# Who issues the regrouping transfers of a self-attention batch: three of six query transfers and two of twelve key transfers go to GpSimd

## The reference

```python
x = x + attn(layernorm(x)); x = x + xattn(layernorm(x), ctx); x = x + ffn(layernorm(x))

def attn(x):                       # 16 heads of 8 channels
    q, k, v = (split_heads(x @ W + b) for W, b in ((Wq, bq), (Wk, bk), (Wv, bv)))
    scores = einsum('bhqd,bhkd->bhqk', q, k) / sqrt(8)
    scores = where(mask, scores, -inf)          # blocks of 64 tokens, and 8 global tokens
    return einsum('bhqk,bhkd->bhqd', softmax(scores), v) @ Wo + bo
```

## Time and profile before

| | |
|---|---|
| median of 3 runs | 567.36 us (565.86 to 570.26) |
| profiled execution | 572.98 us, of which 571.1 us is the span |
| PE / PEld busy | 85% / 64% |
| DVE busy | 71% |
| ACT busy | 52% |
| POOL busy | 51% |
| DMA engines' share in the self attention | 0.38 to 0.61, batch by batch |

### The profile page before, as it was taken

How to read it: one execution, slowest core, us unless ns; L and a number is a source line. 1 busy time by engine, 2 the same in 40 slices (tenths; PEclk the granted TensorE clock), 3 DMA queues, 4 the chain that set the end, 5 groups by cost and what they waited for, 6 DMA issues and landing times. The chain is left out here.

```text
span 571.1 us, 16500 instructions
## 1 busy us (share of the span) xinstructions
PE 487.5 (85%) x5675; PEld 363.8 (64%) x5675; DVE 408.1 (71%) x1245; ACT 297.4 (52%) x757; POOL 288.6 (51%) x540
## 2 busy tenths in 40 slices
PE   1978989899989899878989999999867999999810
PEld 1756666667666666546767777677644888888610
DVE  7567989999888888867987898788472343433337
ACT  2573665555656665425664666465424534444237
POOL 5543434433333343101276788777772477777720
PEclk9997999999999999979997999899988999999985
DMA  6626343545655656216232333322125443343159
GB/s 192 111 53 136 62 63 62 110 107 108 109 108 101 112 103 137 64 47 139 65 80 71 98 85 99 89 73 81 33 67 144 114 113 111 110 115 94 53 173 291
DMA packets 96002, 58.30 MB, mean 102 GB/s; under 512 B 24560, under 2 KB 92224, under 8 KB 95920
## 3 DMA queue, kind: packets, MB, share of 16 engines
q1 hardware_dynamic: 74448, 40.00, 30.3%
q10 hardware_dynamic: 16896, 7.34, 6.5%
q0 software_dynamic: 4576, 9.91, 5.2%
HBM read 20.83 MB, written 17.50 MB: 67 GB/s over the span
## 5 line engine op out<-in xcount | busy, mean ns | idle before, releaser
L507 POOL TENSOR_SCALAR veps<-mv 128x2 f32<-128x2 f32 x48 | 10.8, 225 | 159.3 <-issue 101.4
L1278 ACT ACTIVATE probs<-ps 128x512 f32<-128x512 f32 x128 | 73.2, 602 | 12.1 <-PE ps L1658 10.0
L602 POOL DMA_INDIRECT expert_in<-xn,sloti x64 | 65.6, 1025 | 17.9 <-issue 17.9
L1133 DVE TENSOR_TENSOR eh<-ps,sg 128x256 f32<-128x256 f32 x40 | 17.0, 425 | 59.1 <-ACT sg L1482 58.1
L761 DVE TENSOR_REDUCE nmax<-ps 128x8 f32<-128x512 f32 x64 | 42.5, 686 | 18.9 <-PE ps L1593 18.8
L655 POOL DMA_INDIRECT expert_out<-ey,xt x40 | 38.3, 958 | 27.6 <-DVE ey L1140 17.1
L761 DVE TENSOR_REDUCE mparts<-ps 128x8 bf16<-128x512 f32 x64 | 43.3, 685 | 6.3 <-PE ps L1648 5.9
L1593 PE MATMUL ps<-kbd,qs 96*64 96x128 bf16 x512 | 38.1, 293 | 4.5 <-DMA qs<-part 2.5
L2005 PE MATMUL ps<-wgu,turned 128*128 x160 | 41.2, 380 | 0.0
L1476 ACT COPY turned<-ps 128x512 f32<-128x512 f32 (+1 forms) x43 | 23.8, 554 | 27.7 <-PE ps L1998 23.2
L509 POOL TENSOR_TENSOR rstd<-veps,minus_half 128x2 f32<-128x2 f32 x48 | 35.6, 742 | 4.0
(11 more groups left out here) (247 smaller groups left out, 1387.4 us busy)
## 6 DMA issues: line engine op xcount, KB each, us to landing
kbd<-part SPq DMA_DIRECT2D x192, 32.0 KB
qs<-part ACTq DMA_DIRECT2D x93, 64.0 KB
xt<-expert_in SPq DMA_DIRECT2D x64, 72.0 KB
qs<-part SPq DMA_DIRECT2D x51, 64.0 KB
ck_scr<-wgu SPq DMA_DIRECT2D x6, 512.0 KB
ckbd<-ck_scr SPq DMA_DIRECT2D x16, 192.0 KB
kbd<-part SPq DMA_DIRECT2D x48, 64.0 KB
wgu<-in_L_ffn_gate_up_w SPq DMA_DIRECT2D x4, 512.0 KB, 3.9
```

Source lines behind the costliest of these rows:

```text
L602: pool.indirect_dma_start(xs, bass.IndirectOffsetOnAxis(sloti[b % 3][:, n:n + 1], 0), xn3[b % 3][:, n // TOPK, n % TOPK, :], None).then_in ...
L1278: a_.activation(probs[:, 2 * i:2 * i + 2, :], P2[i % 2][:, :].rearrange("p (j q) -> p j q", j=2), ACT.Exp, scale=SCALE).then_inc(s("probs" ...
```

## The change

From batch 2 on, GpSimd issues five of the 18 transfers: the two query transfers of the second part, the two key transfers of the third part, and the query transfer of the third part, in this order. They add to a semaphore of their own, `lent`. ScalarE keeps the three query transfers of the first part, SP ten key transfers. Whoever waited for `got` now waits for `got` (13 transfers a batch) and `lent` (5). Batches 0 and 1 go as before.

```diff
-        GOT = {True: 16 * 3 * NP, False: 16 * NP}
+        GOT = 16 * NP
+        FIRST_LENT, LENT = 2, 5
+        def self_got(n):
+            return 16 * (3 * NP * n - LENT * max(n - FIRST_LENT, 0))
+        def self_lent(n):
+            return 16 * LENT * max(n - FIRST_LENT, 0)
...
-                        if K_PART[i] == k:
+                        if K_PART[i] == k and (b < FIRST_LENT or k < 2):
                             for a in range(2):
                                 sp.dma_start(kbd[p][16 * i + 8 * a:16 * i + 8 * a + 8, :, a, :, :].rearrange("r j k n -> r j (k n)"),
...
-                wait_apart(sp, (s_("got"), GOT[True] * b + GOT[True]))
+                wait_apart(sp, (s_("got"), self_got(b + 1)), (s_("lent"), self_lent(b + 1)))
...
+            def later_parts_regrouped(b, p):
+                at_least(pool, s_("pair"), 4 * (b - 1))
+                for k in (1, 2):
+                    pool.wait_ge(s_("part"), 3 * b + k + 1)
+                    for i in range(NP):
+                        if Q_PART[i] == k:
+                            pool.dma_start(qs[p][16 * i:16 * i + 16, :, :], part[:, k, 0:S]).then_inc(s_("lent"), 16)
+                        if K_PART[i] == k == 2:
+                            for a in range(2):
+                                pool.dma_start(kbd[p][16 * i + 8 * a:16 * i + 8 * a + 8, :, a, :, :].rearrange("r j k n -> r j (k n)"),
+                                               part[64 * a:64 * a + 64, k, S:2 * S]).then_inc(s_("lent"), 16)
...
             def self_body(b, p):
                 if has(b + 1):
                     self_global_heads(b + 1, 1 - p)
+                    if b + 1 >= FIRST_LENT:
+                        later_parts_regrouped(b + 1, 1 - p)
...
-                at_least(act, s_("got"), GOT[True] * b)
+                at_least(act, s_("got"), self_got(b))
+                at_least(act, s_("lent"), self_lent(b))
                 a_.copy(part[:, 0, :], qk[p][:, :]).then_inc(s_("part"), 1)
...
-                if b != 1:
+                if b == 0:
                     queries_regrouped(b, p, 1)
...
                     self_second_part(b + 1, 1 - p)
-                    if b > 0:
-                        queries_regrouped(b + 1, 1 - p, 2)
...
-                    pe.wait_ge(s_("got"), GOT[True] * b + GOT[True])
+                    pe.wait_ge(s_("got"), self_got(b + 1))
+                    at_least(pe, s_("lent"), self_lent(b + 1))
```

More of the change, by code:

```diff
@@ L432, in regroup_cross @@
                              ck_scr[:, :, :, 2 * M * b:2 * M * (b + 1)].rearrange("i r j n -> (i r) j n")).then_inc(w_("ck_put"), 16)
-                sp.wait_ge(c_("got"), GOT[False] * (b + 1))
+                sp.wait_ge(c_("got"), GOT * (b + 1))
             sp.wait_ge(w_("laid_out"), 2)
@@ L1290, in cross_first_part @@
                 if b == 0:
-                    act.wait_ge(s_("got"), GOT[True] * B)
-                at_least(act, c_("got"), GOT[False] * (b - 1))
+                    act.wait_ge(s_("got"), self_got(B))
+                    act.wait_ge(s_("lent"), self_lent(B))
+                at_least(act, c_("got"), GOT * (b - 1))
                 at_least(act, c_("part"), 3 * b)
@@ L1639, in cross_scores @@
                     pe.wait_ge(w_("ck_put"), 16 * (NP + b + 1))
-                    pe.wait_ge(c_("got"), GOT[False] * (b + 1))
+                    pe.wait_ge(c_("got"), GOT * (b + 1))
                     if b == 0:
```

## The result

The changed kernel takes 572.71 us (median of six runs, 571.63 to 579.89), the kernel before 566.84 (six runs, 565.86 to 570.26): 1.0102 times as long, 95% interval 1.0056 to 1.0149. It is 5.9 us slower, about 1%. The profiled execution of the changed kernel took 579.89 us (span 578.1), that of the kernel before 572.98 (span 571.1); both lie 6 to 7 us above their medians.

What follows compares the result with a forecast made beforehand. The prediction took a fixed 12.74 us loop of VectorE and handovers as the bound. VectorE's + 1.1 us and SP's - 0.3 us, other terms 0, gave + 0.8 us: forecast 568 us, range 563.5 to 577.

Steps and rivals of the forecast that it cites:

- The fixed loop of 12.74 us, set by VectorE and handovers: Self attention: each batch is a fixed loop of 12.74 us; at most 1.65 us in eleven batches are transfer stalls.
- ScalarE's relief worth 0: ScalarE before `xnT`: three issues (1.99 us) go, but `xnT` starts only 0.08 us sooner and ScalarE already idles; worth 0.
- GpSimd's price: GpSimd before `veps`: five issues a batch cost 5.82 us, bounds 3.3 to 6.5, ending before `veps`; path cost 0.
- first rival: GpSimd's issues too long, from about 1.3 us each, delaying last query, keys and `rstd`; 576 us at 1.45; chance 0.20.
- VectorE beside the issues, + 1.1 us: VectorE's two L772 copies beside GpSimd's issues: 0.08 us longer a batch, 1.1 us over 14 batches.
- second rival: GpSimd's issues hold off VectorE's two L772 copies: 0.96 us a batch, 13.4 us, 581 us; chance 0.08.
- The landing, 1.38 to 1.78 us: Transfers before the scores: last query lands 1.38 to 1.78 us after its issue, 0.7 to 1.1 us to spare.
- its last keys land that much sooner: SP's key transfers: two fewer issues bring the last keys 1.35 us sooner, slack rising from 0.95 to 2.3 us.
- something else held TensorE: Longest scores stall, 0.94 us at 84.07, 3.33 us after SP's last issue: keys had landed long before, not their fault.
- third rival: Stalls at the scores are late transfers after all; 4.4 us of waits go, `xnT` gains 1.1 us; 562 us; chance 0.12.
- SP's relief, 0.3 us: Scores' stalls: SP's two fewer issues gain 0.3 us, between 0.06 and 1.65 us.
- The collision, taken as 0: 512 KB behind SP's keys starts 1.35 us sooner, delaying GpSimd's last transfers 0 to 1.3 us; within slack, taken as 0.

Runs made afterwards that it cites:

- run of before with the wait ahead: Kernel before, with SP's wait for the batch's transfers put ahead of the zero rows and the 512 KB: 567.63 us against 568.95, ratio 0.998.
- the run with the wait ahead: The changed kernel, with SP's wait for the batch's transfers put ahead of the zero rows and the 512 KB: 569.33 us, 1.002 of the kernel before.
- keys alone and the wait ahead: Kernel before, with only part three's two key transfers on GpSimd and SP's wait ahead of zero rows and 512 KB: 566.30 us against 568.95, ratio 0.993.

## Why the prediction came out as it did

The time lay in the range, 4.7 us above the forecast and on the line of 1%, where I had no change. That it lay in the range is luck in part: the upper end was there for issues of 1.45 us, which did not come. The sum held + 0.8 us where + 5.9 was measured, and the points were these.

*The fixed loop of 12.74 us, set by VectorE and handovers:* right. On-time batches take 12.73 us in all kernels that don't load ScalarE further.

*ScalarE's relief worth 0:* right. `xnT` (L1256) still waits 2.30 us for TensorE, and L1337 idles for 0.44 us, as L1310 did.

*GpSimd's price:* wrong, on the safe side. The bounds were 3.3 to 6.5 us for five, and the issues stand back to back at 0.57 us, below the lower one (GpSimd's operations of 60 to 235 us: count, busy time, mean ns, idle time before them):

```profile
L565 POOL DMA_DIRECT2D qs<-part x39 | 22.2, 570 | 7.4 <-ACT part L1280 7.1 <-issue 0.2
L568 POOL DMA_DIRECT2D kbd<-part x26 | 14.9, 576 | 1.4 <-DVE part L776 1.0 <-issue 0.4
```

The indirect transfers were the wrong neighbour; ScalarE's issue at 0.66 was the near one. So the first rival's mechanism, issues that are too long, did not happen, though its time, 576, came out nearer than the forecast. The sign that I had set for it did show: the scores' loads wait over 0.33 us for keys in 8 of 13 batches, though not for its reason.

*VectorE beside the issues, + 1.1 us:* about the size, by luck, and not the cause. L797 takes 422 ns in the median, as L772 did; 23 of the 26 copies in the window are at that, and of the 1.1 us of the other three, 1.0 are the two beside the memset that the issues pushed back. The second rival falls as I wrote it, and with it what the Trainium skill ("SBUF — State Buffer", on who interferes with whom) would make of these copies beside the issues alone: neither they nor the issues were stretched by more than about 0.1 us. But its other half, that a computing GpSimd instruction holds VectorE off, is in the loss, and I had not asked what the five issues push in front of VectorE.

*The landing, 1.38 to 1.78 us:* this is the step that failed. I took one stall and one dependent transfer for a constant. The landing varies with what is in flight: 1.74 to 4.03 us without GpSimd's transfers, 3.04 to 5.33 with them. With it fell "its last keys land that much sooner": counted from SP's first issue they land 0.5 us later than before. From the earlier trace rows a batch on time leaves the landing 12.74 - 1.92 - 8.09 = 2.73 us with twelve keys, and by the timeline of the change (1.93 and 6.75 us) 4.06 with ten. In the run of before with the wait ahead, the four landings above 2.73 (2.93, 3.23, 3.36, 4.03) are those of batches 6, 9, 4 and 10, the four in which the scores then wait longest, but for the last batch (0.50, 0.69, 0.98 and 1.20 us). From the same error came the sentence that "something else held TensorE" at 84.07: it was a key that landed 3.3 us after its issue. The third rival's reading of the stalls was right, then, but not its outcome. And *SP's relief, 0.3 us*: with the five transfers left out altogether, batches 2 to 14 shrink from 168.47 us to 166.56, that is by 1.9, of which 0.2 are the batch in which VectorE is busy; the rest is about my upper bound of 1.65. But this is what five transfers fewer are worth, not SP's relief by itself.

*The collision, taken as 0:* mis-sized. I looked for it at the 512 KB alone, and asked only whether GpSimd's transfers suffer. It is SP's that land late, batch by batch, and the zero rows and the 512 KB, which no run tells apart, seem to add to it: moving both behind the wait brought the key row from 8.0 to 5.5. *TensorE's clock* had no term in the sum; about 2 us of the profiled loss go with it.

Which landing is the last in a late batch of the change, SP's or GpSimd's, its trace settles: SP's. In the run with the wait ahead SP goes on 0.3 to 0.8 us after GpSimd's last landing in twelve of thirteen batches (with keys alone and the wait ahead 0.3 to 1.5 us), which looks like B; but by the records of the semaphores `got` rose last there too, 0.13 us before SP goes on. So GpSimd's transfers land late, but they are not what the scores wait for. What is not settled: why all five on GpSimd land the last key 0.5 us later than before, and what in the DMA engines is shared.

## What to carry to other kernels

Moving transfers to an idle engine saved issue time here and little else; the last of the same eighteen transfers landed 0.3 us sooner at best, and with all five moved 0.5 us later. Find the landing that comes last, measure how long it takes from issue (put the issuer's wait right behind its issues and read the gap), and ask what the moved transfers do to it, and what the new issues push back on the engine that makes them. A landing read at one quiet place was a lower bound. When the slack is under 1 us, move few transfers (here two keys) and put large stores behind the wait.

## What the runs showed of the hardware

A plain GpSimd transfer of 64 or 128 rows costs the engine 0.57 us of issue, less than ScalarE's 0.66, but landed 2.8 to 6.3 us after its start in this traffic. A memset on GpSimd stretched VectorE's copy from 0.42 to 0.93 us, while issues alone left it at 0.42 to 0.50.

With GpSimd's transfers in flight, the hardware queue can fall silent though it has work. In the late batch above SP's last key was issued at 93.3, yet these are the DMA engines from 93.5 to 95.0 us (40 slices, tenths busy; then the queues: packets, MB, share), where q0 is GpSimd's queue and q1 SP's:

```profile
DMA  9800000977099990000000000004400070303225
...
q0 software_dynamic: 43, 0.08, 48.5%
q1 hardware_dynamic: 12, 0.00, 7.7%
```

and from 95.0 to 95.5 us:

```profile
q1 hardware_dynamic: 127, 0.06, 74.3%
```

For about half a microsecond no engine moves anything, then SP's packets come all at once. So in this stretch it isn't bandwidth that holds them. The Trainium skill ("DMA: Bandwidth & Descriptors", the section "Issuing engines are not separate DMA queues") says that transfers from all issuing engines interleave on the same DMA engines and that starting them from several saves only the time to start them; the landings above agree, at 10.5 to 11.3 us for eighteen transfers, whoever issues them. Its section "Queues, rings and completion order" says that a transfer's semaphore write lands only after every earlier write of that DMA engine, across its queues, which would let GpSimd's data hold back SP's signals; no run here tells that from a delay of the data itself.
